# The head of an attention stage: weights halved on ScalarE, a count product put first, an accumulator zeroed later

## The chip, the cores and the metric

The kernel runs on one core of one Trainium2 chip. The metric is device time of one execution in microseconds (us), the median of several executions. Three executions of the kernel before gave 1027.07, 1027.90 and 1030.37 us.

## The reference

The reference is one transformer layer on x of shape (2, 1024, 256): a first mixture of experts, linear attention with a feed-forward block, then a second attention with 16 heads of 16 columns, a normalisation modulated by a condition, and a second mixture of experts. The change lies at the start of the second attention:

```
def proj(W): return (x @ W.T).reshape(B, S, H, D).transpose(0, 2, 1, 3)
q, k, v = (proj(Wq), proj(Wk), proj(Wv))
scores = jnp.einsum('bhsd,bhtd->bhst', q, k) * scale
scores = jnp.where(mask[None, None, :, :], -jnp.inf, scores)
attn = jax.nn.softmax(scores, axis=-1)
out = jnp.einsum('bhst,bhtd->bhsd', attn, v)
```

The mask hides a column of keys where it is true. The kernel works only on those tiles of 128 keys in which some key is not hidden (live tiles).

## The kernel before, in words

Every fp32 operand of a product is kept as two halves: a high half, rounded to the format that TensorE takes, and a low half, the fp32 value less the high half. A product is then three matmuls per 128 rows of contraction (high by high, high by low, low by high).

The engines run their own instruction lists, written out by hand, and meet through semaphores. The second attention (`stage_attention`, L1482) is one block that all engines enter together. Ahead of its loop over live tiles it has a head, and this is what each engine does there:

- TensorE (L1656 on) still has four of the eight query products to make, units 4 to 7, six matmuls each. `query_product` of unit u waits until VectorE has taken the low half of unit u-4 (semaphore `qlo`), since both use the same PSUM bank. Behind unit 4 comes one small matmul (L1671), which sums over all partitions how many keys of each tile are not hidden (`keys`, made by VectorE at L2154). Behind unit 6, `turn_tile` (L1661) transposes the first live tile of x.
- ScalarE (L1942 on) loads its table for exponentials with a first small one, then writes zeros into the accumulator `acc` (128 x 4352, L1944), and only then takes the high halves of units 4 to 7 (`query_high`, L779). After unit 4 it copies the first live tile of x (`copy_tile`, L1935), for which VectorE must have published the list of live tiles (`counted`). After unit 6 it takes the high half of the transposed tile (`tile_hi`, L1940).
- VectorE (L2152 on) counts (L2153 to L2154, L2166), makes a reciprocal and a penalty column (L2167, L2168), and takes the low half of unit 0 (`query_lo`, L2159). It then waits for the count product (`cnt_ps`) and works out the list of live tiles (L2171 to L2185), with `query_lo(1)` in it. Then come `query_lo(2)`, three copies of the key weights into `wk[0]` (L2189, three copies side by side since the keys are stacked three times), `query_lo(3)`, six tiny instructions (L2193 to L2198), `query_lo(4)`, the three low halves of the key weights (L2201) with `query_lo(5)` to `query_lo(7)` and `tile_lo` (L2163) between them, both halves of the value weights (`weights_split`, L739 and L740), and a bf16 identity (L2208). Behind it stand nops that release the loop: `added` at L2209 is the first thing that TensorE waits for in the loop.
- GpSimd (L2076 on) issues 48 DMAs (L2091) that stack the query halves in SBUF, twelve for each of four units of batch and half the heads (`q_in`); it then waits for `zeroed` and writes the rows of ones (L2098). In the loop it rescales `acc` (L2117).
- SyncE loads the mask's tile when `counted` is up (L1628), waits for all the stacked queries (L1633) and then loads what the later stages need (L2449 on).

The loop runs over live tiles; with these inputs it runs once. Its first work on TensorE is `stack_keys` (L1679): 24 matmuls for the first two banks of keys. ScalarE evicts each bank (L1959), VectorE takes the low rows (L2217) and turns the mask to bf16 (L2272), and then the score products (L1713, L1716) start, with maxima by VectorE (L2228). Turned scores (L1752, L1753) and exponentials (L1971) follow once the maxima of a first unit are there.

Of the kernel before, what the change touches and what calls it, by code (L numbers as in the profile page):

```python
# [19 lines left out]
ALU = mybir.AluOpType  # L20
ACT = mybir.ActivationFunctionType
# [8 lines left out]
P = 128  # L30
# [23 lines left out]
def adaln_block(nc, d, out):  # L54

    T, D = d["x"].shape
    B = d["cond"].shape[0]
# [11 lines left out]
    HD = 16  # L69
    NH = D // HD  # L70
    HC = NH // KC
    LW = D + 2
    QT = S // P

    with ExitStack() as ctx:
# [7 lines left out]
        ps = [psum[:, i, :] for i in range(8)]  # L83
        ident = sb("ident", [P, P])
# [651 lines left out]
        def weights_split(dve, ch, pairs, done):  # L736

            for raw, hi, lo in pairs:
                ch.link(dve.tensor_copy(hi, raw))  # L739
                dve.tensor_tensor(lo, raw, hi, ALU.subtract).then_inc(done, 1)  # L740
# [741 lines left out]
        def stage_attention(qs, ks_home, y_tok, v_tok, raw, w_in, wq, wsp, qps, qhi, free, load_ahead, pre, loaded, e2_raw, e2_in):  # L1482

            names = ("qlo", "set", "keys", "keyps", "counted", "ones", "zeroed", "own")
            qlo, cset, cnt_in, cnt_ps, counted, ones_set, zeroed, own_set = (sem(f"at_{x}") for x in names)
# [22 lines left out]
            with ExitStack() as st:  # L1508
                def sbl(name, shape, dt=F32):
                    return st.enter_context(nc.sbuf_tensor(name, shape, dt))  # L1510
# [9 lines left out]
                wv = [sbl(f"at_wv{h}", [P, KC, D], F32R) for h in "hl"]  # L1520
                wk = [sbl(f"at_wk{h}", [P, KC, NP2, CP], F32R) for h in "hl"]
# [2 lines left out]
                pv = spare_raw[:, 0:2 * GT].rearrange("p (n q) -> p n q", n=2)  # L1524
                x32 = sbl("at_x32", [P, B, D])
                pT = sbl("at_pT", [P, 2, HB, GT])
                QE = 2 * KC
                q_hi, q_lo = query_home(v_tok), pT[:, :, :, :].rearrange("p a h t -> p (a h t)").rearrange("p (k t) -> p k t", k=KC)
                ks = ks_home[:, :, :].rearrange("p k t -> p (k t)").rearrange("p (n b i t) -> p n b i t", n=NP2, b=B, i=2)
                acc = sbl("at_acc", [P, B, QT, NH, HD + 1])  # L1530
# [3 lines left out]
                identb = sbl("at_identb", [P, P], BF16)  # L1534
                one = sbl("at_one", [P, P])
# [6 lines left out]
                cnt, rc8, keys = sbl("at_cnt", [P, QT]), sbl("at_rc8", [P, QT]), sbl("at_keys", [P, QT])  # L1542
                pen = sbl("at_pen", [P, QT])
# [34 lines left out]
                ss, r, ss2, sm = (take(NT) for _ in range(4))  # L1578
# [16 lines left out]
                def live_tiles(eng):  # L1595
                    eng.wait_ge(counted, 1)
                    return eng.value_load(n_live[0:1, 0:1], min_val=1, max_val=QT)
# [58 lines left out]
                def _(pe):  # L1656
                    def turn_tile(bank, j):
# [4 lines left out]
                                                    x32[:, b, k * P:(k + 1) * P], ident[:, :])  # L1662
                        last.then_inc(xps, 1)

                    for u in range(QE, 2 * NU):
                        pe.wait_ge(qlo, u - QE + 1)
                        query_product(pe, wq, u, qps)
                        if u == QE:
                            pe.wait_ge(cset, 2)
                            pe.wait_ge(cnt_in, 1)  # L1670
                            pe.matmul(ps[7][:, 0:QT], one[:, :], keys[:, :], start=True, stop=True).then_inc(cnt_ps, 1)  # L1671
                        if u == 2 * NU - 2:
                            turn_tile(ps[4], 0)

# [211 lines left out]
                    for g in range(G + 1):  # L1886
                        if g < G:
                            product(g)
                        if g == 0:
                            pe.wait_ge(gnormed, 1)  # L1890
                            for k in range(KC):
                                last = pe.transpose(ps[6][:, k * E2:(k + 1) * E2], gw[:, k * P:(k + 1) * P],
                                                    ident[0:E2, 0:E2])
# [38 lines left out]
                def _(act):  # L1932
# [5 lines left out]
                    def tile_hi(bank, j):  # L1938
                        act.wait_ge(xps, j + 1)
                        act.activation(xt[0][:, :, :, :].rearrange("p k b t -> p (k b t)"), bank, ACT.Copy).then_inc(xhi, 1)  # L1940

                    act.activation(idle[:, :], ident[:, 0:1], ACT.Exp)  # L1942
                    flat = acc[:, :, :, :, :].rearrange("p b u h e -> p (b u h e)")
                    act.activation(flat, ident[:, 0:1].to_broadcast([P, B * QT * NH * (HD + 1)]), ACT.Copy, scale=0.0).then_inc(zeroed, 1)  # L1944
                    for u in range(QE, 2 * NU):
                        query_high(act, q_hi, u, qps, qhi)
                        if u == 2 * NU - 4:
                            act.wait_ge(counted, 1)
                            copy_tile(0)
                        if u == 2 * NU - 2:  # L1950
                            tile_hi(ps[4], 0)
                    act.nop().then_inc(nm_act, 3)
                    act.nop().then_inc(pvev, 1)
                    act.nop().then_inc(pex, 3)
# [31 lines left out]
                    n = live_tiles(act)  # L1986
# [88 lines left out]
                def _(pool):  # L2075
# [8 lines left out]
                    for unit in range(NU):  # L2084
                        b, c = unit // KC, unit % KC
                        pool.wait_ge(qhi, 2 * unit + 2)
                        for copy, src in enumerate((q_hi, q_hi, q_lo)):
                            if copy == 2:
                                pool.wait_ge(qlo, 2 * unit + 2)
                            for pl in range(HC // 2):  # L2090
                                pool.dma_start(stacked(c * (HC // 2) + pl)[copy * 32:(copy + 1) * 32, b * S:(b + 1) * S],  # L2091
                                               src[pl * 32:(pl + 1) * 32, c, b * S:(b + 1) * S]).then_inc(q_in[unit], 16)
                    pool.wait_ge(zeroed, 1)
                    pool.wait_ge(own_set, 1)
                    pool.wait_ge(qps, 2 * NU)
                    for c in range(KC):
# [26 lines left out]
                    n = live_tiles(pool)  # L2123
# [26 lines left out]
                def _(dve):  # L2150
# [4 lines left out]
                    def query_lo(u):  # L2155
                        b, m, g = query_of(u)
                        sl = slice(g * GT, (g + 1) * GT)
                        dve.wait_ge(qhi, u + 1)
                        dve.tensor_tensor(q_lo[:, m, sl], ps[u % 4], q_hi[:, m, sl], ALU.subtract).then_inc(qlo, 1)  # L2159
# [4 lines left out]
                                          xt[0][:, :, :, :].rearrange("p k b t -> p (k b t)"), ALU.subtract).then_inc(xsp, 1)  # L2164

                    ch.link(dve.tensor_reduce(cnt[:, :], free[:, :, :], AX.X, ALU.add))  # L2166
                    ch.link(dve.reciprocal(rc8[:, :], cnt[:, :]))  # L2167
                    ch.link(dve.tensor_scalar(pen[:, :], rc8[:, :], 0.0, None, ALU.mult))  # L2168
                    query_lo(0)
                    dve.wait_ge(cnt_ps, 1)  # L2170
                    ch.link(dve.tensor_scalar(lv[:, :], ps[7][:, 0:QT], 0.0, None, ALU.is_gt))  # L2171
# [12 lines left out]
                    dve.memset(live_at[:, QT:QT + 1], 0)  # L2184
                    dve.tensor_copy(live_at[:, 0:QT], srt[:, :]).then_inc(counted, 1)  # L2185
                    query_lo(2)
                    wk_raw = raw[:, 1, :, :].rearrange("p k (n r) -> p k n r", r=32)
                    for copy in range(3):
                        last = dve.tensor_copy(wk[0][:, :, :, copy * 32:(copy + 1) * 32], wk_raw)  # L2189
                    ch.link(last)  # L2190

                    query_lo(3)
                    dve.tensor_scalar(bits[:, 0:1], row[:, :], 4, 1, ALU.logical_shift_right, ALU.bitwise_and)  # L2193
                    ch.link(dve.tensor_scalar(bits[:, 1:2], row[:, :], 31, 1, ALU.bitwise_and, ALU.logical_shift_right))
# [2 lines left out]
                    dve.tensor_copy(half_is[:, 1:2], bitf[:, 0:1])  # L2197
                    dve.tensor_scalar(own[:, :], rank[:, :], bitf[:, 1:2], None, ALU.is_equal).then_inc(own_set, 1)  # L2198
                    query_lo(4)
                    for copy in range(3):  # L2200
                        last = dve.tensor_tensor(wk[1][:, :, :, copy * 32:(copy + 1) * 32], wk_raw,  # L2201
                                                 wk[0][:, :, :, copy * 32:(copy + 1) * 32], ALU.subtract)
                        query_lo(5 + copy)
                        if copy == 1:
                            tile_lo(ps[4], 0)
                    ch.link(last)
                    weights_split(dve, ch, [(raw[:, 2, :, :], wv[0][:, :, :], wv[1][:, :, :])], wsp)
                    ch.link(dve.tensor_copy(identb[:, :], ident[:, :]))  # L2208
                    dve.nop().then_inc(added, 1)  # L2209
                    dve.nop().then_inc(red, 3)  # L2210
                    dve.nop().then_inc(nm_dve, 3)
# [42 lines left out]
                    def normalise(j, unit):  # L2254
# [9 lines left out]
                                          rc[:, :, :].unsqueeze(3).to_broadcast([P, QT, HC, HD]),  # L2264
                                          ALU.mult).then_inc(rows_set, 1)

                    n = live_tiles(dve)
                    with dve.Fori(0, n) as j:
                        dve.wait_ge(added, j * NBT + 1)
# [234 lines left out]
```

## Time and profile before

| | |
|---|---|
| median of three executions | 1027.9 us |
| the profiled execution | 1029.43 us, of it in the span 1027.7 us |
| mean granted TensorE clock | 0.947 of full speed |
| PE busy | 886.8 us, 86% of the span |
| DVE busy | 747.3 us, 73% |
| ACT busy | 394.8 us, 38% |
| POOL busy | 425.7 us, 41% |

All times in the views are microseconds from the start of the span, unless they are marked ns. PE is TensorE's matmuls, PEld its weight loads, DVE VectorE, ACT ScalarE, POOL GpSimd, SP SyncE; a q behind the name is the engine's sequencer or DMA queue. An idle time in brackets names the instruction that ended it. A chain of waits is followed back from the last instruction of the kernel, at each step to what released it. PEclk is the clock that TensorE was granted, as a share of 2.4 GHz; 0.50 is 1.2 GHz.

### The profile page before, as it was taken

What the parts mean: (1) busy time and instruction counts of PE and PEld (TensorE: products, weight loads), DVE (VectorE), ACT (ScalarE), POOL (GpSimd) and SP (SyncE); (2) the same over time, 40 slices, a digit from 0 to 9 for tenths busy, and PEclk for the clock granted to TensorE, in tenths of its full rate; (3) what the DMA queues carried; (4) which work ended last, traced back from release to release, by engine and by line L of the source; (5) the groups of instructions that cost most, each with busy time, mean ns of one, the idle gap of its engine ahead of it and who ended that gap; (6) DMA issues with size and microseconds to landing.
All of it is one profiled execution on the core that took longest, in us unless ns stands there. A gap on an engine that the chain in (4) does not pass through costs nothing. (4 is left out here: it accounts for less than half of the span.)

```text
span 1027.7 us, 17852 instructions
## 1 busy us (share of the span) xinstructions
PE 886.8 (86%) x5607; PEld 756.1 (74%) x5616; DVE 747.3 (73%) x1449; ACT 394.8 (38%) x746; POOL 425.7 (41%) x489
## 2 busy tenths in 40 slices
PE   4399999999937676799988689988899999999998
PEld 1399999999936565587777655536688888888887
DVE  5888888888826878767876766628677777767676
ACT  4356666666414332413344245568511111111110
POOL 3177777777720224275533722220133333333332
PEclk9599999999978888899989899999999999999999
DMA  8336213135143000050003920000000100101002
GB/s 267 110 98 201 96 41 123 41 124 175 41 126 124 1 0 1 12 186 1 1 1 60 192 68 1 1 1 27 6 17 15 31 21 25 29 17 31 15 0 82
DMA packets 50300, 61.80 MB, mean 60 GB/s; under 512 B 8015, under 2 KB 37769, under 8 KB 50249
## 3 DMA queue, kind: packets, MB, share of 16 engines
q1 hardware_dynamic: 43464, 43.85, 13.9%
q0 software_dynamic: 6336, 17.31, 7.0%
q8 instruction: 26, 0.43, 0.2%
q14 instruction: 26, 0.21, 0.1%
q10 hardware_dynamic: 448, 0.01, 0.0%
HBM read 47.26 MB, written 7.60 MB: 53 GB/s over the span
## 5 line engine op out<-in xcount | busy, mean ns | idle before, releaser
L2145 POOL TENSOR_TENSOR kTh<-at_acc,kTh 128x512 fp32r<-128x512 f32 x68 | 88.2, 1297 | 257.1 <-DVE kTh L2323 257.1
L2071 ACT ACTIVATE at_acc<-psum 128x512 f32<-128x512 f32 x68 | 40.8, 601 | 240.0 <-PE psum L1873 240.0
L2405 DVE SCALAR_TENSOR_TENSOR y<-psum,at_pT,y 128x256 f32<-128x256 f32 x272 | 112.3, 476 | 0.1
L1915 PE MATMUL psum<-at_wkh,kTh 128*128 128x256 f32 x544 | 107.7, 282 | 3.0 <-DVE y L2405 3.0
L1873 PE MATMUL psum<-act_hi,at_wkh 128*128 128x512 f32 x272 | 108.5, 399 | 0.3 <-ACT at_acc L2071 0.3
L1873 PE MATMUL psum<-act_hi,at_wkl 128*128 128x512 f32 x272 | 107.6, 396 | 0.0
L1873 PE MATMUL psum<-act_lo,at_wkh 128*128 128x512 f32 x272 | 107.5, 395 | 0.0
L2320 DVE TENSOR_TENSOR at_acc<-psum,at_acc 128x512 f32<-128x512 f32 x68 | 47.0, 692 | 74.3 <-PE psum L1873 60.9
L444 ACT ACTIVATE e_u<-psum,e_bias 128x256 f32<-128x256 f32 x152 | 63.8, 472 | 95.9 <-PE psum L343 86.9
L1915 PEld LDWEIGHTS psum<-at_wkh,kTh 128*128 128x128 f32 x544 | 88.8, 190 | 7.0 <-DVE y L2405 3.0
L1915 PE MATMUL psum<-at_wkl,kTh 128*128 128x256 f32 x272 | 76.5, 281 | 0.0
L2228 DVE TENSOR_REDUCE at_mn<-psum 128x4 f32<-128x512 f32 x64 | 43.0, 688 | 25.7 <-PE psum L1716 25.2
L1873 PEld LDWEIGHTS psum<-act_hi,at_wkl 128*128 128x128 f32 x272 | 51.4, 189 | 12.8
L1873 PEld LDWEIGHTS psum<-act_hi,at_wkh 128*128 128x128 f32 x272 | 51.2, 188 | 9.8 <-ACT at_acc L2071 0.8
L1873 PEld LDWEIGHTS psum<-act_lo,at_wkh 128*128 128x128 f32 x272 | 51.3, 188 | 9.6
L353 PE MATMUL psum<-e_w3h,e_h2h 128*128 (+1 forms) x160 | 47.9, 299 | 8.7 <-issue 8.4
L1915 PEld LDWEIGHTS psum<-at_wkl,kTh 128*128 128x128 f32 x272 | 51.7, 190 | 2.8
L1361 POOL TENSOR_TENSOR qpl<-ff_h32sb,qph 128x512 fp32r<-128x512 f32 x24 | 33.9, 1416 | 45.1 <-DVE qph L1392 45.1
L690 DVE CAST e_h2h<-e_u 128x512 fp32r<-128x512 f32 x38 | 32.5, 856 | 26.9 <-ACT e_u L444 26.7
L1971 ACT ACTIVATE at_pT<-psum 128x512 f32<-128x512 f32 x64 | 37.8, 600 | 29.7 <-PE psum L1753 29.6
L505 POOL DMA_INDIRECT y_rows<-e_yo,e_destnow x40 | 42.1, 1052 | 9.5 <-issue 9.5
L353 PE MATMUL psum<-e_w3l,e_h2h 128*128 (+1 forms) x160 | 45.9, 287 | 0.0
(498 smaller groups left out, 2839.5 us busy)
## 6 DMA issues: line engine op xcount, KB each, us to landing
e_raw<-in_W SPq DMA_DIRECT2D x16, 512.0 KB, 6.9
e_raw<-in_W SPq DMA_DIRECT2D x8, 1024.0 KB
y<-in_x SPq DMA_DIRECT2D x4, 512.0 KB, 9.5
v_tok<-in_xT SPq DMA_DIRECT2D x4, 512.0 KB, 8.1
y<-y_rows SPq DMA_DIRECT2D x4, 512.0 KB, 7.4
v_tok<-y_rows SPq DMA_DIRECT2D x4, 512.0 KB, 8.4
v_tok<-in_x SPq DMA_DIRECT2D x4, 512.0 KB, 8.9
e_raw<-in_w_gate SPq DMA_DIRECT2D x16, 128.0 KB, 2.1
```

Of the source, the lines that this page charges most:

```text
L353: last = pe.matmul(ps[4][:, j * D:(j + 1) * D], h2[a][:, k, j * P:(j + 1) * P], w3[b][:, bass.ds(slot, 1), k, :].rearrange("p s d -> p (s ...
L444: act.activation(u[:, c // 2, c % 2, :], ps[c // 2][:, (c % 2) * ET:(c % 2 + 1) * ET], ACT.Relu, bias=bias12[:, layer, e, c % MC:c % MC + ...
L505: pool.indirect_dma_start(out=y_rows, out_offset=bass.IndirectOffsetOnAxis(ap=of[:, j:j + 1], axis=0), in_=yo[:, j, :], in_offset=None).th ...
L1361: pool.tensor_tensor(hh[1][:, s % HS, :], h32[:, s % 2, :], hh[0][:, s % HS, :], ALU.subtract).then_inc(hsp, 1)
L1873: last = pe.matmul(bank[:, :], e2_w[par][a][:, o + k * H2:o + (k + 1) * H2], actT[b][:, k, g * GT:(g + 1) * GT], start=n == 0, stop=n == 3 ...
L1915: last = pe.matmul(ps[4 + j][:, 0:D], hh[a][:, s % HS, j * P:(j + 1) * P], e2_w[par][b][:, OD:OD + D], start=n == 0, stop=n == 2)
L1971: act.activation(pT[:, t % 2, k, :], ps[3 + s % 3], ACT.Exp, scale=SCALE).then_inc(pex, 1)
L2071: act.activation(sl_sb[:, s % 2, :], ps[s % 2][:, :], ACT.Silu).then_inc(esil, 1)
L2145: pool.tensor_tensor(hh[1][:, s % HS, :], h32[:, s % 2, :], hh[0][:, s % HS, :], ALU.subtract).then_inc(hsp, 1)
L2228: dve.tensor_reduce(mn[:, unit % 2, u, h2 * HB:(h2 + 1) * HB], ps[a % 3].rearrange("p (h t) -> p h t", t=P), AX.X, ALU.max).then_inc(red, 1)
L2320: dve.tensor_tensor(h32[:, s % 2, :], ps[2 + s % 2][:, :], sl_sb[:, s % 2, :], ALU.mult).then_inc(h32d, 1)
L2405: dve.scalar_tensor_tensor(out=y[:, i, :], in0=ps[4 + j][:, 0:D], scalar=comb[:, i, bass.ds(2 * t + out_s // G, 1)], in1=y[:, i, :], op0=A ...
```

## The change

The matmul that counts live keys stands ahead of all four query products. On ScalarE the zeroing of `acc` moves from the front to behind the last query high half, and in its old place stand three copies into `wk[0]`, one into `wv[0]` and the bf16 identity, each a counted step of `zeroed`. VectorE loses these copies and waits for the fifth of them ahead of the first low half of the key weights. GpSimd's wait for `zeroed` goes from 1 to 6. The reciprocal and the penalty column move behind VectorE's nops, ahead of the loop.

```
@@ TensorE
+                    pe.wait_ge(cset, 2)
+                    pe.wait_ge(cnt_in, 1)
+                    pe.matmul(ps[7][:, 0:QT], one[:, :], keys[:, :], start=True, stop=True).then_inc(cnt_ps, 1)
                     for u in range(QE, 2 * NU):
                         pe.wait_ge(qlo, u - QE + 1)
                         query_product(pe, wq, u, qps)
-                        if u == QE:
-                            pe.wait_ge(cset, 2)
-                            pe.wait_ge(cnt_in, 1)
-                            pe.matmul(ps[7][:, 0:QT], one[:, :], keys[:, :], start=True, stop=True).then_inc(cnt_ps, 1)
@@ ScalarE
                     act.activation(idle[:, :], ident[:, 0:1], ACT.Exp)
-                    flat = acc[:, :, :, :, :].rearrange("p b u h e -> p (b u h e)")
-                    act.activation(flat, ident[:, 0:1].to_broadcast([P, B * QT * NH * (HD + 1)]), ACT.Copy, scale=0.0).then_inc(zeroed, 1)
+                    act.wait_ge(w_in, 48)
+                    for copy in range(3):
+                        act.activation(wk[0][:, :, :, copy * 32:(copy + 1) * 32], wk_raw, ACT.Copy).then_inc(zeroed, 1)
+                    act.activation(wv[0][:, :, :], raw[:, 2, :, :], ACT.Copy).then_inc(zeroed, 1)
+                    act.activation(identb[:, :], ident[:, :], ACT.Copy).then_inc(zeroed, 1)
                     for u in range(QE, 2 * NU):
                         query_high(act, q_hi, u, qps, qhi)
...
                         if u == 2 * NU - 2:
                             tile_hi(ps[4], 0)
+                    flat = acc[:, :, :, :, :].rearrange("p b u h e -> p (b u h e)")
+                    act.activation(flat, ident[:, 0:1].to_broadcast([P, B * QT * NH * (HD + 1)]), ACT.Copy, scale=0.0).then_inc(zeroed, 1)
@@ GpSimd
-                    pool.wait_ge(zeroed, 1)
+                    pool.wait_ge(zeroed, 6)
@@ VectorE
                     ch.link(dve.tensor_reduce(cnt[:, :], free[:, :, :], AX.X, ALU.add))
-                    ch.link(dve.reciprocal(rc8[:, :], cnt[:, :]))
-                    ch.link(dve.tensor_scalar(pen[:, :], rc8[:, :], 0.0, None, ALU.mult))
                     query_lo(0)
                     dve.wait_ge(cnt_ps, 1)
...
                     query_lo(2)
-                    wk_raw = raw[:, 1, :, :].rearrange("p k (n r) -> p k n r", r=32)
-                    for copy in range(3):
-                        last = dve.tensor_copy(wk[0][:, :, :, copy * 32:(copy + 1) * 32], wk_raw)
-                    ch.link(last)
-
                     query_lo(3)
...
                     query_lo(4)
+                    dve.wait_ge(zeroed, 5)
                     for copy in range(3):
                         last = dve.tensor_tensor(wk[1][:, :, :, copy * 32:(copy + 1) * 32], wk_raw,
                                                  wk[0][:, :, :, copy * 32:(copy + 1) * 32], ALU.subtract)
...
                     ch.link(last)
-                    weights_split(dve, ch, [(raw[:, 2, :, :], wv[0][:, :, :], wv[1][:, :, :])], wsp)
-                    ch.link(dve.tensor_copy(identb[:, :], ident[:, :]))
+                    dve.tensor_tensor(wv[1][:, :, :], raw[:, 2, :, :], wv[0][:, :, :], ALU.subtract).then_inc(wsp, 1)
                     dve.nop().then_inc(added, 1)
...
+                    ch.link(dve.reciprocal(rc8[:, :], cnt[:, :]))
+                    ch.link(dve.tensor_scalar(pen[:, :], rc8[:, :], 0.0, None, ALU.mult))
                     n = live_tiles(dve)
                     with dve.Fori(0, n) as j:
```

## Rows read from the trace of the kernel before

**Rows 1.** The page: the chain that ended last, by engine and by line.

```profile
PE 36%; DVE 5%; ACT 2%; issue 2%; DVEq 0%; ACTq 0%
```

**Rows 2.** The chain of waits, 555 to 577 us: start, length, what; xN merges N instructions.

```profile
556.00 0.21 DVE at_rc L2167
...
556.45 0.70 DVE at_pT L2159
...
557.20 1.66 PE psum L767 x6
...
562.38 1.02 DVE at_wkh L2189 x3
...
569.62 0.34 DVE at_wvh L739
...
570.68 0.15 DVE at_identb L2208
...
570.86 0.03 DVEq L2209
...
571.12 5.42 PE psum L1679 x24
```

**Rows 3.** The timeline of DVE: start, length, operation, [idle before <- what ended it].

```profile
555.57 0.27 DVE L2154 TENSOR_REDUCE at_keys<-rows 128x8 f32<-128x64 f32 x1
...
559.02 0.17 DVE L2171 TENSOR_SCALAR at_lv<-psum 128x8 f32<-128x8 f32 x1 [1.87 <-PE psum L1671]
...
561.62 0.17 DVE L2185 CAST at_liveat<-at_srt 128x8 int32<-128x8 f32 x1
...
564.74 0.68 DVE L2159 TENSOR_TENSOR at_pT<-psum,v_tok 128x512 f32<-128x512 f32 x1
...
575.30 1.40 DVE L2217 SCALAR_TENSOR_TENSOR act_hi<-psum,at_half,act_hi 32x512 fp32r<-32x512 f32 x2 [4.47 <-ACT act_hi L1959]
```

**Rows 4.** The timeline of ACT.

```profile
556.58 0.20 ACT L1942 ACTIVATE at_idle<-ident 128x1 f32<-128x1 f32 x1
556.69 3.82 ACT L1944 ACTIVATE at_acc<-ident 128x4352 f32<-128x4352 f32 x1
...
562.51 0.64 ACT L1935 ACTIVATE at_x<-y 128x512 f32 x1 [1.52 <-DVE at_liveat L2185]
...
565.98 0.60 ACT L779 ACTIVATE v_tok<-psum 128x512 fp32r<-128x512 f32 x1 [0.75 <-PE psum L767]
574.00 1.26 ACT L1959 ACTIVATE act_hi<-psum,at_half 96x512 fp32r<-96x512 f32 x2 [7.43 <-PE psum L1679]
```

**Rows 5.** The timeline of PE.

```profile
558.70 0.28 PE L1671 MATMUL psum<-at_keys,at_one 128*128 128x8 f32 x2
560.94 0.50 PE L767 MATMUL psum<-act_hi,at_wqh 128*128 128x512 f32 x1 [1.96 <-DVE at_pT L2159]
...
565.54 0.40 PE L767 MATMUL psum<-act_hi,at_wql 128*128 128x512 f32 x1
571.12 0.50 PE L1679 MATMUL psum<-at_xth,at_wkh 128*96 128x256 f32 x1 [5.18 <-DVEq L2209]
...
577.67 0.39 PE L1713 MATMUL psum<-at_mb,at_identb 128*128 128x512 bf16 x1 [1.15 <-DVE at_mb L2272]
...
583.52 0.28 PE L1679 MATMUL psum<-at_xtl,at_wkh 128*96 128x256 f32 x1
583.64 0.28 PE L1679 MATMUL psum<-at_xth,at_wkl 128*96 128x256 f32 x1
```

**Rows 6.** Stretches of 1 us: length, busy PE, PEld, DVE, ACT, POOL, PEclk, DMA.

```profile
569.00:570.00 1.00, 0.00 (x0) 0.00 (x0) 0.97 (x4) 0.00 (x0) 1.00 (x2) 0.87 1.32 209
...
581.00:582.00 1.00, 1.00 (x8) 0.85 (x6) 0.53 (x1) 0.00 (x0) 0.96 (x2) 0.50 1.37 258
```

**Rows 7.** The timelines of POOL and of SP's DMA queue.

```profile
581.43 4.01 POOL L2098 CAST act_hi<-at_own 16x1024 fp32r<-16x1024 f32 x4
...
589.95 0.56 SPq L2449 DMA_DIRECT2D cd_cT<-in_condT  x1
```

More of the change, by code:

```diff
@@ L1526, in stage_attention @@
                 pT = sbl("at_pT", [P, 2, HB, GT])
+                wk_raw = raw[:, 1, :, :].rearrange("p k (n r) -> p k n r", r=32)
                 QE = 2 * KC
```

## The prediction

> **What bounds the kernel now.** I read the page's chain first: over the whole span TensorE is the chain for 36%, VectorE for 5% [rows 1], and nearly all of it lies in loops that this change doesn't touch. So the change is worth what it shortens the way from the start of the attention block (555.3 us) to its loop, less what is lost behind it. The chain of waits in that stretch runs along VectorE: its small counting instructions, the low half of unit 0 (556.45), one query product on TensorE with the count product behind it, the list of tiles, the key weights, a row of low halves, the value weights and the identity, up to the nop at 570.86 that releases the loop; TensorE starts there at 571.12 [rows 2]. The timelines show the others' room. VectorE has one pause, 1.87 us, for the count product [rows 3]. TensorE has ended its last query product at 565.94 and idles 5.18 us [rows 5]. ScalarE is done at 566.58 and idles 7.43 us, until the first bank of keys stands at 574.00 [rows 4]. So what leaves VectorE here ends the head earlier by its own length, until another engine is late.
>
> **What goes, step by step.**
> - Reciprocal and penalty: they hold the low half of unit 0 from 556.00 to 556.45 [rows 2], 0.45 us. Behind the nops they take the same 0.45 us, where VectorE idles 4.47 us before its first work in the loop [rows 3]: nothing. Without that cover they would cost 0.45 again.
> - The count product first. It needs `keys`, ready at 555.84 [rows 3]. Its two matmuls take 0.28 us, and VectorE read them at 559.02, 0.32 after the first had started [rows 3, 5]. I give its first weight load and both matmuls 0.6 us: ready about 556.45, while the low half of unit 0 runs to 556.70 on the new times. The pause of 1.87 us goes. If the product came as late as 557.0, 0.3 of it would stay. TensorE loses nothing, it idles there.
> - Three key copies: 1.02 us on the chain; the value weights' high half: 0.34; the identity, 570.68 to 570.86: 0.18 [rows 2].
>
> Sum: 0.45 + 1.87 + 1.02 + 0.34 + 0.18 = 3.86 us. VectorE's nop moves from 570.86 to 567.00, TensorE's loop from 571.12 to 567.26.
>
> **What is added, and who waits.** ScalarE gets four copies of 128x512 and one of 128x128 ahead of `query_high(4)`. This trace shows no such weight copy on ScalarE. The nearest row is the copy of x, SBUF to SBUF with as many elements, 0.64 us; from below the eviction of 0.60, from above twice the 0.64, if writing in pieces of 32 were slow; for the identity something between the 0.20 of the one-column activation and 0.64 [rows 4]. I take 4 x 0.64 + 0.3 = 2.9 us, in place of the 3.82 of the zeroing [rows 4]: ScalarE is free at 556.69 + 2.9 = 559.6, 0.8 us sooner than before. VectorE's new wait for these copies stands behind `query_lo(4)`, which moves from 564.74 to about 564.74 - 0.45 - 1.87 - 1.02 = 561.4 [rows 2, 3], and ends at 562.0: 2.4 us after the copies, so the wait costs nothing. With copies of twice the price they end at 562.2 and the wait itself costs 0.2.
>
> Narrower are the query halves. TensorE makes unit 4 from 556.75 to 558.4 (1.66 us [rows 2]). ScalarE takes its high half 559.6 to 560.2. The list of tiles is up at 561.79 - 2.32 = 559.5 [rows 3]; the copy of x came 0.8 us after it [rows 3, 4] and can start at 560.3, at worst 561.0, and ends by 561.6. High half 5 follows by 562.2; VectorE asks for it at 562.6. Units 6 and 7 wait for low halves 2 and 3, which end at about 560.1 and 560.8, so TensorE ends unit 6 at 561.7, the transposes by 562.3 and unit 7 by 563.7; high halves 6 and 7 end at 563 and 564.2, and VectorE asks at 563.8 and 565.6. No wait, with 0.4 us of slack at the worst place. Twice the copy price would turn that into about 2 us of wait.
>
> The zeroing now runs on ScalarE from 564.2 to 568.0 (3.82 us [rows 4]). Its reader on GpSimd reaches its wait at 581.43 [rows 7]. Behind it on ScalarE stand three nops, the read of the number of tiles and the loop. The first bank of keys stands at 574.00 - 3.86 = 570.1 [rows 4], 2.1 us later. The cover is real but not wide: an idle ScalarE hid the loop's entry before. Between nothing and the whole idle time of 7.43 us bounds that entry; I take 0.8, the delay of the other register read.
>
> Absolute times that do not move: SyncE passes its wait for the stacked queries before 589.95, and GpSimd's rows of ones end at 585.44 [rows 7]; both are needed only by the turned scores at about 601.7, now 597.8.
>
> **The clock.** It is granted at 0.50 from 569.87 (0.87 of the stretch of 1 us that ends at 570) [rows 6], after TensorE had idled 3.9 us, and the 24 key matmuls run at 1.2 GHz: 5.42 us [rows 2]. At 2.4 GHz such matmuls follow each other at 0.12 us [rows 5], 2.9 us for 24. So 2.5 us are at stake. The gap shrinks from 5.18 to 563.7..567.3, 3.6 us, just under the 3.9 us of idling after which the clock had fallen. Later it fell again (0.50 at 581) though TensorE's pauses were only 1.15 us and shorter, the score products being sparse [rows 5, 6]. That second fall tells me that a gap need not be long to bring the clock down; I keep the clock's cost as it is, and take the gain of 2.5 us as a rival.
>
> By the Trainium skill (TensorE: Matmul & The Clock Gate, "Why this matters for your kernels"), it is idle gaps between bursts that drop TensorE to half rate, and the advice is to leave none. By that rule a gap that remains still drops it, which gives the forecast's 1024.0, and the second fall, with hardly a gap before it, shouldn't have come; this trace has it.
>
> **Forecast.** 3.86 us off the profiled execution: 1029.43 - 3.86 = 1025.6 (span 1023.8). That execution is 1.5 us above the median of the three runs; from 1027.9 it is 1024.0, and this I forecast, with 1022.7 to 1025.3 as its own range for the clock's whims.
>
> **Rivals.**
> - *The clock survives the shorter gap.* For it: 3.6 us against 3.9. Against it: the second fall. A further 2.5 us off, 1024.0 - 2.5 = 1021.5; ScalarE, free at 568.8 with its loop entry, would then meet the first bank at about 568.7, so no more than that.
> - *Part of the gain is given back in front of or behind the loop's start:* ScalarE's copies in pieces of 32 are slow and high half 5 becomes the wait (up to 2 us), or one more stretch at 1.2 GHz like the second one, which is over by 583.52, where the matmuls again follow at 0.12 [rows 5]; from 580 on that is 3.5 us and costs its half, 1.7. Time 1024.0 + 2 = 1026.0. For it: the slack of 0.4. Against it: the row of 0.64.
> - *ScalarE's loop entry isn't hidden (the other side).* Before, it had 7.43 us of idling to get into the loop; if entering takes them all, it can evict the first bank at 568.0 + 7.4 = 575.4, not at 574.00: slower than before by 1.4 us, 1029.3. It decides once entry takes more than 6 us. Against it: nothing of the trace shows so long an entry, VectorE's was under its 4.47 us.
>
> **Chances.** Forecast 0.50, clock 0.20, given back 0.24, loop entry 0.06. A difference under 0.3% (3.1 us) can't be told from none; faster than that means under 1024.8: three quarters of the forecast's half (0.38), the clock's 0.20, and a little of the given back, 0.60 in all. Slower means over 1031: 0.03, from the last rival with a bad clock. Same: 0.37. The range goes from the clock's case with some luck, 1021, to 1027, between the given-back case and the last.
>
> **What would show it.** Right: TensorE's L1679 starts 3.9 us earlier after the block's start; no pause of VectorE between the low half of unit 0 and the nop; ScalarE's weight copies at 0.64 each; the zeroing ends ahead of the first bank. Wrong: VectorE waits for ScalarE inside the head, ScalarE's first L1959 comes later than its bank, or the score phase is longer than before by as much as the head is shorter.

## Result and profile after

The changed kernel takes 1022.6 us (median of six executions, 1021.44 to 1023.31) against 1028.13 us before (six, 1027.07 to 1030.37): ratio 0.994, 95% interval 0.9929 to 0.9951. The forecast was 1024.0 in 1021 to 1027. In a later comparison (e4) the same two kernels stood at 1022.97 and 1029.99, ratio 0.9933 (0.992 to 0.9945).

The profiled execution of the changed kernel took 1021.63 us, its span 1019.6. The page's chain is nearly as in [rows 1]:

```profile
PE 36%; DVE 5%; ACT 3%; issue 2%; DVEq 0%; ACTq 0%
```

The chain of waits in the head, beside [rows 2]. The block now starts at 553.65; that it starts 1.6 us sooner is not the change's (the code ahead of it is the same, and in the 14 profiles of this study the block starts anywhere from 553.2 to 558.0). So all that follows is counted from the block's start.

```profile
554.13 0.22 DVE at_cnt L2171
554.35 0.02 issue
554.37 0.69 DVE at_pT L2164
555.07 0.08 DVE at_lv L2174
...
557.65 1.27 DVE at_pT L2164 x2
...
559.64 0.59 DVE at_pT L2164
560.23 0.60 DVE at_wkl L2200
...
564.35 0.69 DVE at_wvl L2206
565.04 0.14 issue
565.17 2.86 PE psum L1679 x12
568.03 0.02 issue
568.06 0.04 ACT act_hi L1964
```

The reader is to see that the count product, the key copies, the value weights' high half and the identity have left the chain, that VectorE goes from one piece to the next without a pause of any size, and that the chain crosses to TensorE at 565.17. That is 11.52 us behind the block's start, against 571.12 - 555.28 = 15.84 before: 4.32 us less.

The timeline of VectorE at the places of [rows 3]:

```profile
553.94 0.27 DVE L2159 TENSOR_REDUCE at_keys<-rows 128x8 f32<-128x64 f32 x1
...
554.98 0.15 DVE L2174 TENSOR_SCALAR at_lv<-psum 128x8 f32<-128x8 f32 x1
...
557.64 1.28 DVE L2164 TENSOR_TENSOR at_pT<-psum,v_tok 128x512 f32<-128x512 f32 x2
...
559.55 0.68 DVE L2164 TENSOR_TENSOR at_pT<-psum,v_tok 128x512 f32<-128x512 f32 x1
...
563.74 0.68 DVE L2164 TENSOR_TENSOR at_pT<-psum,v_tok 128x512 f32<-128x512 f32 x1
564.35 0.68 DVE L2206 TENSOR_TENSOR at_wvl<-pj_raw,at_wvh 128x512 fp32r<-128x512 f32 x1
564.94 0.20 DVE L2265 RECIPROCAL at_rc<-at_cnt 128x8 f32<-128x8 f32 x1
...
569.35 1.40 DVE L2215 SCALAR_TENSOR_TENSOR act_hi<-psum,at_half,act_hi 32x512 fp32r<-32x512 f32 x2 [4.00 <-ACT act_hi L1964]
```

`at_lv` (L2174) no longer waits for the count product, and the reciprocal lies in the pause of 4.00 us ahead of the loop's work. ScalarE, beside [rows 4]:

```profile
555.06 1.66 ACT L1945 ACTIVATE at_wkh<-pj_raw 128x512 fp32r<-128x512 f32 x3
556.63 0.61 ACT L1946 ACTIVATE at_wvh<-pj_raw 128x512 fp32r<-128x512 f32 x1
557.15 0.29 ACT L1947 ACTIVATE at_identb<-ident 128x128 bf16<-128x128 f32 x1
557.35 0.57 ACT L779 ACTIVATE v_tok<-psum 128x512 fp32r<-128x512 f32 x1
558.58 0.63 ACT L1935 ACTIVATE at_x<-y 128x512 f32 x1 [0.65 <-issue]
...
562.42 3.82 ACT L1956 ACTIVATE at_acc<-ident 128x4352 f32<-128x4352 f32 x1
568.06 1.26 ACT L1964 ACTIVATE act_hi<-psum,at_half 96x512 fp32r<-96x512 f32 x2 [1.82 <-PE psum L1679]
```

The copies take 557.44 - 555.06 = 2.4 us (forecast 2.9), the zeroing ends at 566.24, and the first eviction follows its bank at once. On TensorE the pause ahead of the loop is 3.29 us, not 5.18 [rows 5]:

```profile
555.12 0.50 PE L767 MATMUL psum<-act_hi,at_wqh 128*128 128x512 f32 x1 [0.40 <-DVE at_pT L2164]
...
565.17 0.50 PE L1679 MATMUL psum<-at_xth,at_wkh 128*96 128x256 f32 x1 [3.29 <-DVE at_wvl L2206]
...
569.29 0.28 PE L1679 MATMUL psum<-at_xth,at_wkl 128*96 128x256 f32 x1
571.75 0.61 PE L1713 MATMUL psum<-at_mb,at_identb 128*128 128x512 bf16 x1 [2.19 <-DVE at_mb L2272]
```

The clock, in stretches of 1 us as in [rows 6] (PEclk, the third figure from the end, is the mean over the stretch):

```profile
564.00:565.00 1.00, 0.00 (x0) 0.00 (x0) 1.00 (x3) 1.00 (x1) 1.00 (x3) 0.89 1.26 197
565.00:566.00 1.00, 0.83 (x4) 0.86 (x5) 0.31 (x3) 1.00 (x1) 1.00 (x3) 0.50 1.28 229
...
568.00:569.00 1.00, 1.00 (x10) 1.00 (x9) 0.00 (x0) 0.94 (x2) 1.00 (x3) 0.90 1.35 213
...
572.00:573.00 1.00, 0.79 (x3) 0.40 (x2) 0.97 (x3) 0.00 (x0) 1.00 (x4) 0.50 1.21 205
```

It falls ahead of the loop's start, at 564.78 (0.89 is the mean of a stretch with 0.78 us at full and the rest at half clock), when TensorE has idled 2.9 us. The 24 key matmuls run partly at full clock: 565.17 to 569.57, 4.4 us in place of 5.42. It falls again in the score phase, at 571.6, and there stays at half for 6.8 us, twice the 3.4 us of before. From the first key matmul to the exponentials this profile is therefore not shorter than the first of before but 0.45 us longer (31.63 against 31.18 below). The copying of the stacked queries didn't move and wasn't needed earlier: SyncE's next load is at 588.51, 34.9 us behind the block's start (34.7 before), still 8 us ahead of the first exponential.

To see where the whole difference lies, each profile is cut at five events of its timelines: block start, first L1679, first exponential of the turned scores, the next stage's table load, the first accumulation of the last experts, the end. Times in us:

| kernel | to L1679 | to exp | to table load | to experts | to end | block start to end |
|---|---|---|---|---|---|---|
| before | 15.83 | 31.18 | 89.25 | 55.29 | 280.83 | 472.4 |
| before again (e8) | 16.63 | 31.61 | 89.23 | 53.77 | 279.89 | 471.1 |
| changed | 11.51 | 31.63 | 89.18 | 53.76 | 279.91 | 466.0 |
| changed again (e4) | 11.58 | 29.92 | 89.19 | 53.74 | 279.88 | 464.3 |
| e1 count only | 13.87 | 30.60 | 89.23 | 55.38 | 279.89 | 469.0 |
| e2 weights only | 14.80 | 28.48 | 90.78 | 53.74 | 279.46 | 467.3 |
| e3 zeroing in front | 13.65 | 31.61 | 89.20 | 53.73 | 279.90 | 468.1 |
| e5 filler | 11.51 | 29.45 | 89.17 | 55.32 | 281.05 | 466.5 |
| e6 values late | 10.97 | 31.16 | 89.15 | 55.33 | 281.28 | 467.9 |
| e7 both | 10.91 | 29.58 | 89.18 | 55.33 | 281.82 | 466.8 |
| e9 filler in before | 15.88 | 30.48 | 89.16 | 53.76 | 281.08 | 470.4 |
| e10 late filler | 11.50 | 30.11 | 89.20 | 53.69 | 280.66 | 465.2 |
| e11 all filler | 11.95 | 29.51 | 89.20 | 53.77 | 279.90 | 464.3 |
| e12 with late values | 11.53 | 29.98 | 89.20 | 53.71 | 279.88 | 464.3 |

The mean of the two profiles of each kernel differs by 471.75 - 465.15 = 6.6 us: 4.7 in the head, 0.6 up to the exponentials (all of it from e4's profile), 0.8 and 0.5 in the later stages.

### The profile page after: what moved, and what is told of

Its sections match the earlier page's. It is cut to its first block and busy times, and to the rows that moved or that the text cites. A ratio compares the mean times of both kernels' runs of the same rounds, so it can differ in the third digit from the quotient of the medians.

```text
span 1019.6 us, 17861 instructions
## 1 busy us (share of the span) xinstructions
PE 883.6 (87%) x5616; PEld 753.3 (74%) x5616; DVE 746.3 (73%) x1444; ACT 395.6 (39%) x751; POOL 424.7 (42%) x489
## 6 DMA issues: line engine op xcount, KB each, us to landing
e_raw<-in_W SPq DMA_DIRECT2D x8, 1024.0 KB, 6.0
```

## Experiments

**e1, the count product alone.** The edit, on the kernel before:

```
+                    pe.wait_ge(cset, 2)
+                    pe.wait_ge(cnt_in, 1)
+                    pe.matmul(ps[7][:, 0:QT], one[:, :], keys[:, :], start=True, stop=True).then_inc(cnt_ps, 1)
                     for u in range(QE, 2 * NU):
...
-                        if u == QE:
-                            pe.wait_ge(cset, 2)
-                            pe.wait_ge(cnt_in, 1)
-                            pe.matmul(ps[7][:, 0:QT], one[:, :], keys[:, :], start=True, stop=True).then_inc(cnt_ps, 1)
```

> The kernel before with one edit: the count product stands ahead of the four query products. Theory (each part is worth what it takes from VectorE's row, and the rest of the 5.5 us comes from the clock): VectorE's pause for the count goes, 1.9 us; 1026.2 us, and block start to the first L1679 15.8 - 1.9 = 13.9 us. Rival (the head's gain is really larger than its terms, since parts help each other): under 1 us alone.

Measured: 1025.27 us, ratio to before 0.9955 (0.9943 to 0.9968); head 13.87 us, 1.96 less than the first profile of before. The pause is gone:

```profile
556.19 0.69 DVE L2158 TENSOR_TENSOR at_pT<-psum,v_tok 128x512 f32<-128x512 f32 x1
556.80 0.15 DVE L2170 TENSOR_SCALAR at_lv<-psum 128x8 f32<-128x8 f32 x1
```

The term is right in the head. The median lies 4.7 us under that of before beside it (1029.99), more than twice the head's gain, so the head isn't the whole of it.

**e2, ScalarE's copies and the late zeroing alone** (the changed kernel with `cnt_ps`'s matmul and the two small VectorE instructions back in their old places).

> The changed kernel with the count product and the reciprocal and penalty back in their old places: only ScalarE's weight copies and the late zeroing are left. Theory: 1.02 + 0.34 + 0.18 = 1.5 us less than before in the head, plus some tenths from the identity's tail; 1026.5 us. Block start to L1679 14.2 us. Rival (the parts only work together): less than 0.5 us.

Measured: 1024.95 us, ratio 0.9956 (0.9941 to 0.9971); head 14.80 us, only 1.03 under 15.83. The reason stands in one row, VectorE's pause for the count product, 2.63 us and not 1.87:

```profile
562.35 0.17 DVE L2177 TENSOR_SCALAR at_lv<-psum 128x8 f32<-128x8 f32 x1 [2.63 <-PE psum L1672]
```

and in a stretch of 1 us in which the clock had fallen under the query product that stands ahead of the count:

```profile
561.00:562.00 1.00, 1.00 (x5) 0.79 (x3) 0.00 (x0) 0.65 (x2) 1.00 (x3) 0.50 0.80 152
```

The second profile of before (e8) has the same pause at half clock, 2.67 us, and a head of 16.63:

```profile
561.51 0.17 DVE L2171 TENSOR_SCALAR at_lv<-psum 128x8 f32<-128x8 f32 x1 [2.67 <-PE psum L1671]
```

Against that profile e2 saves 1.83 us. So in the head the parts add (1.96 + 1.83 + the 0.45 forecast for the small instructions = 4.24, measured 4.32), and the rival falls; what is uneven is the clock under the query product. The medians don't add so: 4.7 us (e1) and 5.0 us (e2) against 7.0 for the whole change beside them (e4).

**e3, the zeroing back in front on ScalarE:**

```
                     act.activation(idle[:, :], ident[:, 0:1], ACT.Exp)
+                    act.activation(flat, ident[:, 0:1].to_broadcast([P, B * QT * NH * (HD + 1)]), ACT.Copy, scale=0.0).then_inc(zeroed, 1)
...
-                    act.activation(flat, ident[:, 0:1].to_broadcast([P, B * QT * NH * (HD + 1)]), ACT.Copy, scale=0.0).then_inc(zeroed, 1)
...
-                    dve.wait_ge(zeroed, 5)
+                    dve.wait_ge(zeroed, 6)
```

> The changed kernel with the zeroing of acc back in front on ScalarE, the weight copies behind it. Theory: ScalarE frees itself 3.8 us later, at 557.4 + 3.8 = 561.2 on the times of the changed kernel's trace, where VectorE wants high half 4 at 559.6 and high half 5 at 560.8; the copy of x and high half 5 follow at 562.4 to 563, so VectorE waits about 2 to 2.5 us in the head: 1024.8 us. Rival (ScalarE has slack enough wherever the zeroing stands): as the changed kernel, 1022.6.

Measured: 1025.62 us (0.996, 0.9945 to 0.9975), 2.65 us above the changed kernel beside it (e4, 1022.97); head 13.65 us, 2.1 more. VectorE waits in one place:

```profile
564.24 0.69 DVE L2164 TENSOR_TENSOR at_pT<-psum,v_tok 128x512 f32<-128x512 f32 x1 [2.05 <-ACT v_tok L779]
```

So the zeroing's new place is what makes the copies on ScalarE free.

**e4, the changed kernel again.** 

> The changed kernel once more, for its spread and a second profile. Theory (the 1.7 us beyond the head's 3.9 are two later stretches at half clock, near 703 and 747 us, that fell where TensorE's work stood before and not where it stands now): the ratio is 0.994 to 0.995 again, and the profile has no half clock between 600 us and the end. Rival (chance): the ratio is nearer 0.996, and such stretches show up in this profile.

Measured: 1022.97 us (1020.88 to 1024.2), ratio 0.9933 (0.992 to 0.9945). No half clock between 600 us and the last 4 us of the span, as in the first profile. That fits the theory; e8 speaks against it. At the loop's start this profile differs from the first one. The clock outlived the pause, 2.10 us here, and fell only at 570.92 (the stretch of 1 us that ends at 571 has 0.96), in the middle of key matmuls that had followed each other at 0.12 us. From there they take 0.41 us each, not 0.28, and follow at 0.21:

```profile
569.48 0.33 PE L1679 MATMUL psum<-at_xth,at_wkh 128*96 128x256 f32 x1 [2.10 <-DVE at_wvl L2206]
...
571.18 0.41 PE L1679 MATMUL psum<-at_xtl,at_wkh 128*96 128x256 f32 x1
```

The 24 took 4.1 us all the same. The exponentials came 29.92 us behind the first of them, not 31.63.

**e8, the kernel before again.** 

> The kernel before once more, for a second profile. Theory (its later stretches at half clock, near 703 and 747 us, belong to where TensorE's pauses stand in this kernel): at least one such stretch between 690 and 760 us again, and block start plus 136 us at the table load of the next stage. Rival (they fall by chance, as often in either kernel): none here.

Measured: 1030.21 us (one execution), and neither late stretch: its columns behind the table load (53.77 and 279.89) are those of the changed kernel. The table load comes 137.5 us behind the block's start. The rival holds here. In the first profile of before, the clock in the two stretches:

```profile
703.00:704.00 1.00, 1.00 (x7) 1.00 (x6) 0.96 (x3) 0.72 (x4) 0.00 (x0) 0.50 0.00 0
...
748.00:749.00 1.00, 1.00 (x6) 1.00 (x6) 1.00 (x3) 0.00 (x0) 0.28 (x1) 0.50 0.00 0
```

**e5, filler in TensorE's pause** (on the changed kernel, behind the last query product):

```
+                    for _ in range(12):
+                        pe.matmul(ps[5], wq[0][:, 0, 0:P], wq[0][:, :, :].rearrange("p k d -> p (k d)"), start=True, stop=True)
```

> The changed kernel with 12 filler matmuls (128x512 of the query weights into an idle PSUM bank, results unused) behind the last query product on TensorE, about 2.8 us in the pause of 3.3 us ahead of the loop. Theory (the pause ahead of the loop is what brings the clock down there): no half clock at the loop's start, the first 24 L1679 take 2.9 us instead of 4.1 to 5.4, ScalarE enters the loop right behind its zeroing: 1.2 to 2 us less than the changed kernel, 1021. Rival (ScalarE's loop entry behind the zeroing, 3.8 us, is then late): ScalarE's first L1964 comes over 1 us after its bank and the gain is under 0.5 us.

Measured: 1024.11 us (0.9949, 0.9936 to 0.9961), no gain. The clock stayed up at the loop's start, and the exponentials began 40.96 us behind the block's start against 43.14 and 41.50; but this profile has a late stretch at half clock, and 1.6 us more ahead of the experts. On ScalarE the rival falls too: the first eviction waited for its bank, not the bank for ScalarE.

```profile
565.00 3.83 ACT L1958 ACTIVATE at_acc<-ident 128x4352 f32<-128x4352 f32 x1
569.42 1.26 ACT L1966 ACTIVATE act_hi<-psum,at_half 96x512 fp32r<-96x512 f32 x2 [0.59 <-PE psum L1681]
```

**e6, the value weights' low half behind the nops:**

```
-                    dve.tensor_tensor(wv[1][:, :, :], raw[:, 2, :, :], wv[0][:, :, :], ALU.subtract).then_inc(wsp, 1)
                     dve.nop().then_inc(added, 1)
...
+                    dve.tensor_tensor(wv[1][:, :, :], raw[:, 2, :, :], wv[0][:, :, :], ALU.subtract).then_inc(wsp, 1)
                     ch.link(dve.reciprocal(rc8[:, :], cnt[:, :]))
@@ TensorE
+                        pe.wait_ge(wsp, 3)
                         for i, (k, (x_, w_)) in enumerate((k, p) for k in range(KC) for p in PASSES):
                             last = pe.matmul(ps[7][:, b * D:(b + 1) * D], xt[x_][:, k, b, :], wv[w_][:, k, :],
...
-                        pe.wait_ge(wsp, 3)
+                        pe.wait_ge(qlo, 2 * NU)
```

> The changed kernel with the value weights' low half (one VectorE instruction) behind the nops that release the loop; TensorE waits for it ahead of the value products instead, and for the eighth query low half ahead of the first key product. Theory (VectorE's row still bounds the head): 0.6 us less in the head, block start to L1679 10.9 to 11.0 us; the median 0.6 lower, which the clock's spread may hide. Rival (TensorE or ScalarE is the bound by now): no change in the head.

Measured: head 10.97 us, as expected, and 1025.17 us (0.9953, 0.9937 to 0.9968) over eleven executions that form two heaps: 1020.72 to 1023.46 (five) and 1025.17 to 1027.77 (six). The profile belongs to the upper heap and has both late stretches. VectorE's row still bounds the head, but the zeroing on ScalarE now bounds what follows:

```profile
567.50 3.83 ACT L1957 ACTIVATE at_acc<-ident 128x4352 f32<-128x4352 f32 x1
571.23 2.39 ACT L1965 ACTIVATE act_hi<-psum,at_half 96x512 fp32r<-96x512 f32 x4
```

No idle time stands ahead of the eviction, and entering the loop cost nothing that can be seen. But the twelfth key matmul, the last of the first bank, began at 569.82, so the bank stood at about 570.1 (estimate, from the 0.32 us between the same two in e9), and the eviction began 1.1 us later, as the zeroing ended. So much of what the shorter head and the key matmuls at full clock had gained is lost there.

**e7, e5 and e6 together.** 

> Both: filler matmuls and the late value weights. Theory: the two add, 1.8 to 2.6 us less than the changed kernel, 1020.5; with 10.9 us of head the zeroing on ScalarE starts to be near its limit. Rival: no better than the filler alone.

Measured: 1024.91 us (0.9959, 0.9946 to 0.9972), head 10.91, both late stretches in the profile. The gains in the head and up to the exponentials (40.49 us behind the block's start) are there and don't arrive at the end.

**e9, 20 filler matmuls in the kernel before,** at the same place. 

> The kernel before with 20 filler matmuls (4.7 us, results unused) in TensorE's pause of 5.2 us ahead of the loop, nothing else. Theory (a good part of what the change brought beyond VectorE's row is that the shorter pause ahead of the loop costs fewer half-clock stretches): block start to L1679 stays 15.8 to 16.6 us, the 24 L1679 take 2.9 to 4 us instead of 4.4 to 5.4, and the median falls by 1 to 2 us against before. Rival (the clock at the loop's start is worth nothing, something later waits anyway): under 0.5 us.

Measured: 1029.05 us, ratio 0.9993 (0.9981 to 1.0005): nothing in the median. Yet the 24 key matmuls ran at full clock:

```profile
563.73 4.71 PE L1675 MATMUL psum<-at_wqh 128*128 128x512 f32 x20
569.12 0.33 PE L1681 MATMUL psum<-at_xth,at_wkh 128*96 128x256 f32 x1 [0.67 <-DVEq L2211]
```

The last of them began at 571.86, so all took 3.0 us in place of 5.4, and the exponentials came 0.7 us earlier than in the first profile of before. Of 2.4 us some 0.7 are left: ScalarE's and VectorE's evictions of the two banks are then the chain, and the clock fell later instead, from 574.7 on. Again the twelve executions form two heaps, 1025.31 to 1027.04 (five, the profiled one among them) and 1028.91 to 1031.66 (seven). The lower heap lies under all 17 executions of before beside it (1027.65 to 1031.12). So the filler may have gained 2 us or more in some executions and nothing in the others; why is open.

**e10, filler in two later pauses** of the changed kernel (4 matmuls behind the gate weights' transposes, 8 ahead of the loop over experts):

```
                             last.then_inc(gps, 1)
+                            for _ in range(4):
+                                pe.matmul(ps[5], wq[0][:, 0, 0:P], wq[0][:, :, :].rearrange("p k d -> p (k d)"), start=True, stop=True)
...
                     pe.wait_ge(zin, 1)
+                    for _ in range(8):
+                        pe.matmul(ps[4], wq[0][:, 0, 0:P], wq[0][:, :, :].rearrange("p k d -> p (k d)"), start=True, stop=True)
```

> The changed kernel with filler matmuls in two later pauses of TensorE: 4 behind the transposes of gate weights, 8 ahead of the loop over experts. Theory (these two pauses bring the clock down in some executions, by where they happen to fall, 1.2 us each): no half clock between 650 us and the last experts, table load to end 333.6 us in the profile, the runs' spread smaller and their upper end lower, median at or under the changed kernel's. Rival (the changed kernel has no such stretches in most executions, the filler only stands in the way): no gain, or some tenths slower.

Measured: 1022.96 us (1022.18 to 1025.05; ratio 0.9943, 0.9929 to 0.9957): the changed kernel's time. No late stretch, but e4 has none either. From the table load to the end it is 334.35 us, not 333.6, and the spread is hardly smaller (2.9 us against 3.3 in e4).

**e11, the filler of e5 and of e10.** 

> The changed kernel with the 12 filler matmuls ahead of the attention loop and the late ones. Theory: the filler ahead of the loop was worth about 1.3 us in the attention (block start to table load 130.1 against 130.7 and 132.3) and lost it again to the late stretches; with these filled too it shows: 1 to 2 us under the changed kernel, about 1021.3. Rival (the late loss has another cause than the clock): about 1024, as with the first filler alone.

Measured: 1021.18 us (1018.86 to 1023.85), ratio 0.992 (0.9903 to 0.9936). The lowest median of the study, but its interval overlaps that of the changed kernel in e4 (0.992 to 0.9945), so that it beats it isn't shown. Its head is 11.95 us, 0.4 longer than without filler, for the reason that e12 shows.

**e12, e11 with late value weights and 10 filler matmuls in the head.** 

> Late value weights, 10 filler matmuls ahead of the attention loop, and the late filler. Theory: 0.6 us of head and the clock's stretches: 1020.5, with a narrow spread, under both kernels. Rival: as e11 or as the changed kernel, within 0.5 us.

Measured: 1022.78 us (1019.25 to 1024.29), ratio 0.9929 (0.9912 to 0.9946), as the changed kernel. Its head is 11.53 us, not 10.9: the clock had fallen under query products (from 560.6 to 564.0), the filler started late and was itself what the loop waited for:

```profile
567.24 2.46 PE L1675 MATMUL psum<-at_wqh 128*128 128x512 f32 x10
569.53 0.28 PE L1681 MATMUL psum<-at_xth,at_wkh 128*96 128x256 f32 x1
```

## Why the prediction was right, and by how much it was short

**The number.** 1022.6 us lies in the range, but 0.1 us under the forecast's own 1022.7 to 1025.3, and a little nearer to the clock rival's 1021.5 than to 1024.0. The mechanism forecast for the head is the one that the runs show. It doesn't explain the 1.6 us by which the median fell further than forecast.

**The head.** Forecast 3.86 us, measured 4.32 between the two first profiles. The terms: reciprocal and penalty 0.45 (0.45 forecast), from the first low half to `at_lv` 2.57 - 0.61 = 1.96 (1.87), the key copies 1.73 - 0.60 = 1.13 (1.02), the value weights' high half 1.05 - 0.61 = 0.44 (0.34), the identity and what follows it 1.13 - 0.82 = 0.31 (0.18). Each of the last four is about 0.1 us too small for one reason: I took lengths of pieces of the chain, where the distance between the starts of what stands before and behind also holds the gap of an instruction that waits for the one before it. The rows of before for the distances 1.73 and 1.05:

```profile
561.69 0.68 DVE L2159 TENSOR_TENSOR at_pT<-psum,v_tok 128x512 f32<-128x512 f32 x1
...
563.42 0.69 DVE L2159 TENSOR_TENSOR at_pT<-psum,v_tok 128x512 f32<-128x512 f32 x1
...
568.94 0.68 DVE L2159 TENSOR_TENSOR at_pT<-psum,v_tok 128x512 f32<-128x512 f32 x1
...
569.99 0.69 DVE L740 TENSOR_TENSOR at_wvl<-pj_raw,at_wvh 128x512 fp32r<-128x512 f32 x1
```

**The cover.** Reciprocal and penalty are hidden (pause of 4.00 us). The weight copies cost ScalarE 2.4 us, not 2.9, and VectorE never waits for a high half. The zeroing ends 1.8 us ahead of the first bank. e6 shows where this ends: with 0.6 us less on VectorE and the key matmuls at full clock, the first bank waits for ScalarE.

**The rivals.** ScalarE's loop entry: refuted, in e6 the eviction begins as the zeroing ends. Slow copies: refuted, 0.55 us each in a row of three. Part given back: not in the medians; but in the first profile the longer second stretch took back the 1.0 us that the key matmuls had gained, and 0.45 us more. The clock surviving the gap: in part. In the first profile it didn't, the first keys ran at 1.2 GHz; in e4 it did, and fell 1.4 us later. In neither were the 2.5 us gained: the 24 matmuls took 4.4 and 4.1 us, not 2.9. What was said for this rival rests on a misreading. 0.87 in [rows 6] is the mean of the stretch, so the clock fell at 569.74, when TensorE had idled 3.8 us, not 3.9; and in the changed kernel it fell after 2.9 us. The pause of 3.6 us (measured 3.29) was no safer for being under 3.9.

**The step that was short** is "I keep the clock's cost as it is". The median fell by 5.5 us, and by 7.0 in the second comparison, not by 3.9. In the table the means are 6.6 apart, 4.7 of them in the head.

Part of the difference lies in the head. The change took TensorE out of VectorE's row: before, VectorE waited for a query product and the count behind it, and that product took 1.66 us or more by the clock (pause 1.87, 2.67 in e8, 2.63 in e2); now no clock reaches the row: in e4 it fell under the query products, from 560.7 to 564.1, and the head is 11.58 us against 11.51. That is 0.4 us on the average of the two profiles of before.

The rest, some 1.9 us, lies behind the head. In all, from the block's start to the last experts, the profiles of before hold 17.1 us at half clock each, those of the changed kernel 10.2 each. That the 1.9 us are this clock is likely from the table: where the column ahead of the experts is 55.3 and not 53.75 us, a stretch at half clock lies there in every case (1.6 us, near the block's start plus 140 to 148 us), and in no other. The last column isn't explained so: in e5, e9 and e10 it is 0.8 to 1.2 us longer, with more half clock only in the last 3 us. But e9 moved one such fall and the median didn't move, and e8 shows that the late stretches come and go in one and the same kernel.

Each execution's mean granted clock is on record: 0.946 on average over the 44 executions of before beside e1 to e12, 0.949 over the twelve of the changed kernel. As time at half clock, 2 x (1 - clock) of the span, that is 111 and 104 us. So the changed kernel does have some 7 us less of it, and not only in the profiled executions. What these 7 us are worth stays open: e5 has 100 us at half clock and is no faster than the changed kernel, and among the 44 of before the time doesn't go with the clock.

By the Trainium skill (TensorE: Matmul & The Clock Gate, "Why this matters for your kernels"), idle gaps between bursts of matmuls are to be avoided once they are longer than a certain length; the prediction tells this advice without that condition. The traces agree in part: in the pause ahead of the loop the clock fell within 5.18, 3.92 and 3.29 us (before, e8, changed) and not within 2.10 us (e4), and filling the pause kept it up at that place (e5, e9); but it also fell where no such gap was (below). The filler was worth nothing in the medians of e5, e7 and e9. In their profiles the clock fell at a later place, and in e9 the evictions were next.

## What to carry to other kernels

A row of small instructions on one engine is priced by the distances between starts, not by their lengths, and by whether another engine's product stands inside it: a tiny matmul ahead of the large ones took out a pause of 1.9 us. The work moved to ScalarE was free only because ScalarE's own long instruction was put behind what others wait for (e3: 2.1 us of head and 2.65 us of the median otherwise). A gain of a few us in a kernel whose TensorE pauses is blurred by the clock in steps of 1 to 2 us; compare profiles section by section before believing a median.

## What was unexpected of the hardware

- Executions of one kernel fall into two heaps, their medians 4.7 us (e6) and 3.3 us (e9) apart. The heaps go with the granted clock: in e6 0.949 to 0.951 in the lower and 0.945 to 0.947 in the upper, in e9 0.947 to 0.952 and 0.945 to 0.948. Between profiles one stage shows a step of 1.6 us, each time with a stretch at half clock in it.
- The clock fell also without a long pause: at 571.6 in the changed kernel, when TensorE had idled 2.0 us; at 580 in [rows 5, 6], with pauses of 1.15 us or less; at 570.92 in e4, 1.4 us into matmuls without any pause.
- GpSimd's pairs of DMA issues took longer than 0.98 us where VectorE's fp32 copies ran beside them, 1.34 us at 562.14 and 1.27 at 569.26 in the profile of before, and 1.20 beside the mask's conversion (576.32), but 0.97 beside its subtractions of two SBUF operands (L2201). The Trainium skill (GPSIMD Engine Reference, "Key points") names as contending for the shared SBUF interfaces VectorE's instructions in a 2-port perf mode and those with two SBUF inputs. Beside the second kind this trace shows no slowing; in which mode the copies ran it doesn't show. In the changed kernel, without the copies, the issues of the head follow each other at 0.96 us:

```profile
557.53 1.01 POOL L2096 DMA_DIRECT2D kTh<-v_tok  x2
558.49 1.02 POOL L2096 DMA_DIRECT2D qph<-v_tok  x2
```
